# Decoder block megakernel, middle stage: rows ahead of the softmax maxima, one split behind the rows, the Gelu table one step sooner

## The reference, cut to what matters

```
x = x + attention_0(layernorm(x))        # 16 heads of 8                 "first", items 0 to 7
x = x + cross_attention_0(layernorm(x))  # one head of 128, keys ctx     CROSS
x = x + expert_ffn(layernorm(x))         # gelu (tanh form), 512 tokens  the expert step
x = x + causal_attention(layernorm(x))   # one head of 128               CAUSAL
x = x + cross_attention_1(layernorm(x))  # 16 heads of 8, keys ctx       LAST
x = x + routed_ffn(layernorm(x))         # all rows light, 128 routed rows heavy
```

## Time and profile before

| | us |
|---|---|
| median of 3 runs (range) | 395.78 (393.95 to 395.92) |
| the profiled execution: its own time | 398.66 |
| its span, first to last instruction | 396.8 |
| busy: PE, DVE, ACT, POOL | 359.0, 311.1, 266.0, 163.9 |

### The profile page before, as it was taken

How to read it: one execution, slowest core, us unless ns; L and a number is a source line. 1 busy time by engine, 2 the same in 40 slices (tenths; PEclk the granted TensorE clock), 3 DMA queues, 4 the chain that set the end, 5 groups by cost and what they waited for, 6 DMA issues and landing times.

```text
span 396.8 us, 9561 instructions
## 1 busy us (share of the span) xinstructions
PE 359.0 (90%) x3232; PEld 210.3 (53%) x3232; DVE 311.1 (78%) x870; ACT 266.0 (67%) x595; POOL 163.9 (41%) x269
## 2 busy tenths in 40 slices
PE   6888999999989979998999978999889889989994
PEld 6764445454444357876447834444444434447564
DVE  5677699889989267895447877898988997479995
ACT  2434788888878756775641757887777887765751
POOL 6763544663400013349101475258667422370001
PEclk9997999999999999998999999999999999999999
DMA  6424133214250000001400002311311300000003
GB/s 220 126 55 116 48 99 99 55 50 131 60 168 2 2 0 3 0 2 41 105 15 1 2 14 69 78 48 40 81 36 49 82 2 3 2 1 2 1 2 106
DMA packets 36054, 20.00 MB, mean 50 GB/s; under 512 B 4150, under 2 KB 35046, under 8 KB 36006
## 3 DMA queue, kind: packets, MB, share of 16 engines
q1 hardware_dynamic: 34982, 17.81, 16.7%
q10 hardware_dynamic: 896, 1.31, 0.9%
q0 software_dynamic: 128, 0.26, 0.2%
HBM read 5.58 MB, written 1.05 MB: 17 GB/s over the span
## 4 chain that ended last, share of the span: by engine, by line
PE 72%; DVE 11%; ACT 7%; issue 6%; POOL 2%; DMA 1%; ACTq 0%; POOLq 0%; DVEq 0%
PE pv_ps L1401 15%; PE s_ps L1355 14%; DVE negmax_sb L974 4%; PE s_ps L1364 4%; PE s_ps L1458 4%; PE prep_ps L1311 4%; PE out_ps L1512 3%; PE s_ps L1694 3%; ACT probT_sb L666 3%; PE s_ps L1480 2%; PE prep_ps L1315 2%; PE s_ps L1540 2%; PE pv_ps L1296 2%; PE s_ps L1530 2%; PE prep_ps L1338 2%
## 5 line engine op out<-in xcount | busy, mean ns | idle before, releaser
L974 DVE TENSOR_REDUCE negmax_sb<-s_ps 128x2 bf16<-128x512 f32 x256 | 165.0, 690 | 39.6 <-PE s_ps L1364 38.9
L666 ACT ACTIVATE probT_sb<-s_ps 128x512 f32<-128x512 f32 x256 | 143.4, 596 | 35.8 <-PE s_ps L1355 32.9
L1355 PE MATMUL s_ps<-stack_sb 63*128 63x256 bf16 x512 | 91.1, 276 | 13.1 <-DVE negmax_sb L974 7.3
L1364 PE MATMUL s_ps<-stack_sb 62*128 62x256 bf16 x512 | 91.4, 277 | 0.6 <-DVE negmax_sb L974 0.6
L1401 PE MATMUL pv_ps<-probT_sb,v_aug_sb 128*32 128x256 f32 x1024 | 70.0, 392 | 0.5 <-ACT probT_sb L666 0.5
L1355 PEld LDWEIGHTS s_ps<-stack_sb 63*128 63x128 bf16 x512 | 31.2, 95 | 69.9 <-ACT probT_sb L666 38.4
L516 POOL TENSOR_SCALAR rstd_sb<-mv_sb 128x2 f32<-128x2 f32 x32 | 7.2, 226 | 105.7 <-DVE mv_sb L950 105.3
L1401 PEld LDWEIGHTS pv_ps<-probT_sb,v_aug_sb 128*32 128x32 f32 x1024 | 27.0, 110 | 26.1 <-issue 13.7
L1364 PEld LDWEIGHTS s_ps<-stack_sb 62*128 62x128 bf16 x512 | 31.0, 95 | 9.7 <-DVE negmax_sb L974 5.4
L689 ACT ACTIVATE qkf_sb<-prep_ps,b_qkv_sb 128x256 f32<-128x256 f32 x56 | 23.9, 470 | 10.5 <-PE prep_ps L1315 10.1
L1223 DVE SCALAR_TENSOR_TENSOR late_sb<-late_sb,level_sb,k_inv_sb 8x256 f32<-8x256 f32 x49 | 23.2, 474 | 1.8
(11 more groups left out here) (207 smaller groups left out, 642.9 us busy)
## 6 DMA issues: line engine op xcount, KB each, us to landing
stack_sb<-parts_sb SPq DMA_DIRECT2D x186, 64.0 KB, 2.1
x_all_sb<-x SPq DMA_DIRECT2D x4, 256.0 KB, 3.0
ctxT_sb<-ctxT ACTq DMA_DIRECT2D x2, 512.0 KB, 7.0
f_w_sb<-f_w SPq DMA_DIRECT2D x2, 512.0 KB, 3.6
out<-x_all_sb SPq DMA_DIRECT2D x4, 256.0 KB, 2.4
d_w_sb<-d_w SPq DMA_DIRECT2D x2, 320.0 KB, 3.6
w_att_sb<-w_att SPq DMA_DIRECT2D x2, 256.0 KB, 4.2
stack_sb<-maxrow_sb ACTq DMA_DIRECT2D x32, 4.0 KB
```

The source lines that it names most:

```text
L666: act.activation(probT[:, c % 8], s2_ps[c % 2][:, :, :], ACT.Exp, scale=DH ** -0.5).then_inc(exp_ready, 1)
L974: dve.tensor_reduce(negmax[:, n % 2, :, max_column(max_head(h))], first_bank(c)[:, :, :], axis=AX.X, op=ALU.max, negate=True).then_inc(max ...
L1355: i = pe.matmul(s2_ps[c % 2][:, k, :], stack[rows, s3, 1, h // 2, k * P:(k + 1) * P], stack[rows, s3, 0, h // 2, :], start=True, stop=True)
L1364: i = pe.matmul(first_bank(c)[:, k, :], stack[rows, s3, 0, hp, k * P:(k + 1) * P], stack[rows, s3, 1, hp, :], start=True, stop=True)
```

## The change

Three edits. On DVE, `ln_apply(i+2)` is written ahead of `softmax_bias(i)` in every middle step. On POOL, `split(B + 2)` gets a wait for the rows of the late loop's fourth item (`xn_ready`). On ACT, the one-column Gelu moves from step B+13 to step B+12.

```diff
@@ POOL, end of the middle @@
                     value_bias(LAST_ITEM)
                     rstd_step_(item(B + AHEAD_C))
+                    pool.wait_ge(xn_ready, item(B + AHEAD_C) + 1)
                     split(pool, B + 2)
@@ ACT, middle @@
+                        if i == FFN_STEP - 1:
+                            act.activation(expo_f[:, :], minus_half[0:B, 0:1], ACT.Gelu_apprx_tanh)
                         if i == FFN_STEP:
-                            act.activation(expo_f[:, :], minus_half[0:B, 0:1], ACT.Gelu_apprx_tanh)
                             f_xnT_copy()
@@ DVE, middle @@
-                        if IS_MID[i]:
-                            softmax_bias(i)
                         for n in ahead(i, 2):
                             if n > B + AHEAD:
                                 ln_apply(n)
+                        if IS_MID[i]:
+                            softmax_bias(i)
```

## The result

The change makes the kernel slower: 398.79 us in the median of 13 runs (396.88 to 402.04) against 395.6 of 13 runs of the kernel before, ratio 1.0095 with a 95% interval from 1.0067 to 1.0123. The ratio, which is that of the means, makes it 3.8 us; the medians differ by 3.2. I had forecast +1.15 and a range of 393.8 to 398.6; the median lies 0.2 above it.

A forecast was written before the change was run, and what follows sets the result against it. The prediction took PE to bound the kernel (72% of the span of the chain that ended last). Its terms, 0.5 + 0 + 0.65 - 0.7 + 1.4 - 0.7, gave +1.15 us, so 396.9 us, range 393.8 to 398.6.

The forecast's parts named there:

- the two signs of a wrong forecast: B+14's exponentials starting less than 0.5 us later against the experts' end, or PE meeting no wait for the stack.
- Ordinary steps: 0: Ordinary CROSS steps: rows delay maxima and exponentials by up to 0.6 us, hidden by 0.64 us of cover; cost 0.
- Step B+1: +0.5: Maxima stand behind rows waiting for a late rstd, so PE waits for exponentials: +0.5 us, bounds 0.3 to 0.6.
- Step B+11: +0.65: POOL's split holds rows and scale, so copies and PE's projection come about 0.9 us later; +0.65, bounds 0 and 1.2.
- Gelu table: -0.7: Earlier load hides in ACT's 1.82 us wait in B+12, PE's f_xnT wait goes: -0.7 us, bounds -0.5 and -0.8.
- the rival of the stalling table: At full clock load and Gelu outlast their cover, B+13's copies wait 1.0 us: sum +2.1, 397.9 us; chance 0.05.
- Step B+14: +1.4: Late rstd and POOL's value bias hold the rows, exponentials come 1.7 us late: +1.4 us, bounds 0.85 and 1.7.
- the rival with a third stretch at 1.2 GHz: PE idling in B+14 and B+15 drops the clock again, costing up to 1.7 us; 398.4 us; chance 0.14.
- Seam: -0.7: Shorter rows bring maxima 1.1 us earlier, the later split makes PE wait 0.5 for its stack: -0.7, bounds -0.5 and -1.1.

## Why the prediction was wrong

The direction of the sum was right and its size was not. One term had the wrong sign, and it accounts for the difference: without it I had +1.85, and rows and table together measure +1.8 ± 0.35. That they agree so well is in part luck: for the rows alone I had +2.55 and their runs give +1.9 ± 0.35, and the table, which I had at -0.7, takes 0.1 ± 0.5 off that. Neither of the two signs of a wrong forecast that I had named appeared: they asked whether PE waits for the stack, not how long and against which arrival.

**Ordinary steps: 0.** Right. With the three dear steps in the old order 0.2 ± 0.35 is left, and the waits of B+7 and B+8 bought nothing.

**Step B+1: +0.5.** Right. From the transposes of B to those of B+3 before takes 10.11 us (146.08 to 156.19) and the change 10.59 (145.07 to 155.66): +0.48, nearly all of it in the first step (3.80 against 3.38).

**Step B+11: +0.65.** The mechanism is right, the size that of full clock, which I had named (0.9): from B+7 to B+11 15.47 us against 14.51, +0.96. The rows slipped in between POOL's passes and the projection came late. The scale started at 182.85, behind the first 1.10 us of L415, 0.05 before its end (181.75 + 1.15), and took 0.17. In the sum it met the pass 0.04 before its end, so the pass held it for next to nothing in either; it stood behind maxima that were late by themselves. The Trainium skill (SBUF — State Buffer, Who interferes with whom) says that `tensor_scalar` can use the port pair shared with GpSimd and that whoever comes second waits; the 1.43 of the rows here agree with it.

**Gelu table: -0.7.** In the profiles, right only beside the rows; the times do not show it even there (see Open). From B+11 to B+13 the two together take 29.96 against 30.84, -0.88; the table alone 30.83, since the rows of B+15 are "just too late for the full gain", in fact for all of it. The load stood for 1.28 and the next ACTIVATE came 0.01 behind its end (185.65 + 1.28 = 186.93, 186.94). The drain that the Trainium skill adds (ScalarE: Activation LUTs, What ACT_TABLE_LOAD costs) does not show in this row either. The q/k copies of B+13 came at 187.05, straight behind the load and its Gelu: they were held for a little, as in the rival of the stalling table, and that rival's loss did not follow, as the passage was faster all the same.

**Step B+14: +1.4.** Right: 5.03 against 3.59 from B+13 to B+14, +1.44, of which 0.10 comes back by B+17 (9.97 and 9.98 against 10.08). The wait of PE is 1.16, where I had said about 1.2. The clock did not fall there, so the rival with a third stretch at 1.2 GHz did not come about.

These are 0.48 + 0.96 - 0.88 + 1.34 = +1.90 in the profiles.

**Seam: -0.7.** This is the step that failed; it measures +1.6 ± 0.35. Three things were in it. The maxima did come early, and by more than the 1.1 of the rows: the first row copy stands at 10.10 in place of 12.34, since the clock stayed up. But what the stack delays is counted from PE's arrival, and I compared the new landing with an arrival of before, 246.38, that had the slow stretch of the earlier trace rows in it. I had written that a clock that does not fall "gains nothing more, because PE would only reach that wait sooner". That holds for the changed kernel, and I did not see that it turns against the change: an old seam with its clock up (the profile of the table with the rows of B+13) gets that microsecond. It comes to the group 14.05 behind the weighted sum of B+17 in place of 15.02, and its stack lands 0.55 late. Against that old seam the whole change loses 1.0 and 1.5 to the end of the span (165.40 and 165.93 against 164.43). With a stretch at 1.2 GHz on either side the split's wait alone loses 1.1 and 1.9 (166.61 and 167.29 against 165.52 and 165.44). The 1.6 lies among these four. The second profile of before, with 7 us at 1.2 GHz and 167.01, has no counterpart among them; beside it the same two would read +0.3 and -0.4. The third is the landing. I let the last DMA land 9.1 behind the first issue (236.7 to 245.8), as it did in the profile of before. In all four profiles with the split's wait and 12 DMAs on SP one issue took 1.09 to 1.61 in place of 0.60, and the last landing came 9.6 to 10.2 behind the first issue. So 0.5 to 1.1 of PE's waits of 2.2 to 2.8 is a term that I had too small. And 0.82 of the waits PE has at this group in any case, for DVE, as the run with 2 DMAs on POOL shows: the stack itself delays it by 1.4 to 2.0 (15.15 to 15.72 against 13.77), where I had 0.5.

So the differences "are of one stage, so I add them to the median" was the general form of the error: a term that is set by a race between PE and a DMA is not the same in an execution that lies 2.7 us above the median because PE was slowed.

**Open.** The table with its rows gained 0.88 in the passage from B+11 to B+13 at full clock, and nothing in the times: neither in the kernel that has rows early in B+13 alone nor between the rows with the table (+1.8) and without it (+1.9). The rows' three steps lose 0.48 + 0.96 + 1.34 = 2.78 in the passages, and the rows alone 1.9 ± 0.35 in the times. The runs don't say where the two differences go. Why the clock fell behind the stack's wait in both profiles of the POOL edit alone, and in neither of the whole change, isn't settled, and how often it does in the timed runs isn't seen. So the seam's 1.6 isn't divided further between the wait and the clock.

## What to carry to other kernels

Before a producer is moved later to give a consumer room, look at what the producer's output is waited for, and compare its landing with the earliest arrival that the waiting engine can have, not with that of an execution in which this engine was slowed. When several DMAs in a row on one queue stand between a result and its reader, spread two of them over an idle queue first; here that turned a loss of 1.6 us into a gain of 0.9. And an instruction moved ahead in a fixed order costs time in the steps where its own input is late (B+1, B+14) or its engine's port is held (B+11), so move it step by step and not in the whole loop.

## What the runs showed that I had not expected

- The clock behind an idle PE. In eight of nine profiles with the old seam PE stood 1.3 us for DVE and the granted clock then went to half within a few us; in one it did not. Behind waits of 2.2 and 2.7 us for the stack it fell, behind waits of 2.3 and 2.8 us it stayed at 2.4 GHz. How long PE stands does not alone decide it.
- SP's DMA issue takes 0.60 us. But in eight of the twelve profiles in which SP issues the 12 DMAs of this stack in a row, one of them took 1.09 to 1.61, and the last landed 9.6 to 10.2 behind the first issue; in the other four, the profile of the prediction among them, 9.0 to 9.1. Four of the eight are old seams, so the split's wait does not make it. Nor is it a DMA issue of ACT just before: in the second profile of before the long one starts at 238.80 (1.54), and ACT issues none between 232 and 243.54. Nothing was run to find the cause.
